# Four-layer graph network on one core: linear before aggregation in layer 0, counting sort on TensorE, 128-row cells, and a regrouped edge loop

## What is computed

```python
# layer 0
h_self = h @ W_self.T
neigh_mean = segment_sum(h[src], dst) / maximum(deg, 1)
x += layernorm(h_self + neigh_mean @ W_neigh.T + bias) * gamma + beta
# layer 1: two graph convolutions with edge weights, then row-normalised
# layer 2: message per edge from h[src] and 128 attributes, sum by dst, GRU cell, batch norm
m = relu(concat(h[src], edge_attr) @ W1.T + b1) @ W2.T + b2
agg = segment_sum(m, dst)
# layer 3
x += segment_sum(h[src] * edge_weight1, dst) @ W_3.T + b_3
```

## Time and profile before

| | |
|---|---|
| time, three runs | 1702.89, 1706.38 (median), 1710.26 us |
| profiled execution, first to last instruction | 1705.3 us |
| DVE / PE / POOL / ACT busy | 1190.8 / 1349.3 / 812.9 / 610.3 us |
| mean granted TensorE clock | 0.924 |
| to the first cell scatter | 104 us |
| the build | 367 to 663 us |
| the edge loop | 1021 to 1366 us |

### The profile page before, as it was taken

One profiled execution on the slowest core, in us unless ns is written; L12 is line 12 of the kernel. 1 busy time (PEld: TensorE's weight loads), 2 busy tenths in 40 slices (PEclk: granted clock), 3 DMA queues, 4 the chain that ended last, 5 costly groups with the idle time before them and its releaser, 6 DMA issues.

```text
span 1705.3 us, 20878 instructions
## 1 busy us (share of the span) xinstructions
PE 1349.3 (79%) x4114; PEld 711.6 (42%) x4114; DVE 1190.8 (70%) x1940; ACT 610.3 (36%) x1561; POOL 812.9 (48%) x985
## 2 busy tenths in 40 slices
PE   0277190039999999599899887899899899999899
PEld 0243140024444443344587533444444344444575
DVE  8999863029999999645624727788888756666632
ACT  0132010037666672000200116777777622222310
POOL 2547776766666665066766615666666500000000
PEclk9989585569999999699999999999999999999899
DMA  8363131010000004333432536756666600000220
GB/s 349 129 249 114 61 113 38 1 31 0 0 0 0 0 0 159 133 96 108 123 90 86 158 129 210 242 176 183 181 188 187 192 31 1 0 1 0 62 86 36
DMA packets 81183, 168.18 MB, mean 99 GB/s; under 512 B 15436, under 2 KB 37838, under 8 KB 77556
## 3 DMA queue, kind: packets, MB, share of 16 engines
q1 hardware_dynamic: 53140, 103.63, 17.5%
q0 software_dynamic: 25472, 59.97, 12.4%
q10 hardware_dynamic: 2528, 4.06, 0.9%
HBM read 116.17 MB, written 51.44 MB: 98 GB/s over the span
## 4 chain that ended last, share of the span: by engine, by line
PE 40%; issue 25%; POOL 15%; DVE 10%; DMA 7%; POOLq 1%; SPq 1%; ACT 1%; DVEq 0%; ACTq 0%
PE pb L985 16%; PE pb L936 16%; POOL dst_rows L654 7%; POOL cell_rows L607 5%; PE pb L1170 4%; DMA arena<-p_rows,gidx 3%; DVE arena L1378 3%; DMA arena<-dst_rows 3%; DVE arena L1233 2%; POOL arena L676 1%; PE pb L922 1%; DVE arena L1261 1%; DVE arena L1228 1%; PE pb L1107 1%; DVE arena L1341 1%
## 5 line engine op out<-in xcount | busy, mean ns | idle before, releaser
L676 POOL DMA_INDIRECT arena<-p_rows,gidx x184 | 188.4, 1024 | 103.3 <-issue 54.6
L985 PE MATMUL pb<-arena 128*128 128x384 f32 x368 | 140.8, 507 | 117.1 <-POOL arena L627 109.1
L654 POOL DMA_INDIRECT dst_rows<-ering,gidx x168 | 168.1, 1001 | 127.2 <-issue 73.6
L607 POOL DMA_INDIRECT cell_rows<-tiles,gidx x168 | 169.8, 1011 | 73.6 <-issue 45.9
L1107 PE MATMUL pb<-arena 128*128 128x512 f32 x368 | 196.6, 617 | 1.3 <-ACT arena L821 1.3
L717 ACT ACTIVATE arena<-iota,cellm 128x128 f32<-128x128 f32 x368 | 127.7, 394 | 194.0 <-DMA cellm<-cell_rows 113.5
L1462 DVE TENSOR_TENSOR arena<-pb,arena 128x512 f32<-128x512 f32 x184 | 126.5, 687 | 65.6 <-DMA arena<-p_rows,gidx 59.6
L1347 DVE TENSOR_TENSOR arena<-iota,cellm 128x256 f32<-128x256 f32 x92 | 107.6, 1170 | 87.6 <-issue 87.6
L985 PEld LDWEIGHTS pb<-arena 128*128 128x128 f32 x368 | 64.1, 192 | 193.1 <-ACT arena L722 166.3
L985 PE MATMUL pb<-tiles,arena 128*128 128x384 f32 x368 | 140.1, 504 | 5.7
L827 ACT ACTIVATE high<-arena 128x512 fp32r<-128x512 f32 x184 | 115.3, 627 | 72.0 <-DVE arena L1462 59.0
(11 more groups left out here) (206 smaller groups left out, 2351.2 us busy)
## 6 DMA issues: line engine op xcount, KB each, us to landing
dst_rows<-arena SPq DMA_DIRECT2D x6, 2046.0 KB, 18.1
arena<-dst_rows SPq DMA_DIRECT2D x46, 264.0 KB
ering<-in_edge_attr_dram SPq DMA_DIRECT2D x41, 256.0 KB
arena<-adj SPq DMA_DIRECT2D x10, 640.0 KB, 4.0
arena<-in_x_dram SPq DMA_DIRECT2D x18, 256.0 KB, 5.2
arena<-in_L_gnn_W_hh_dram SPq DMA_DIRECT2D x3, 1024.0 KB
wt_hh<-ws SPq DMA_DIRECT2D x3, 1024.0 KB, 5.9
arena<-in_L_gnn_W_ih_dram SPq DMA_DIRECT2D x3, 1024.0 KB
```

What stands on the lines that cost most here:

```text
L607: nc.gpsimd.indirect_dma_start(cell_rows[:, :], bass.IndirectOffsetOnAxis(gidx[:, k:k + 1], 0), cring[:, k, :], None).then_inc(c_scattered ...
L654: nc.gpsimd.indirect_dma_start(dst_rows[:, :], bass.IndirectOffsetOnAxis(gidx[:, k:k + 1], 0), ering[:, k, :], None).then_inc(e_scattered[ ...
L676: nc.gpsimd.indirect_dma_start(rows[:, k, :], None, p_rows[:, :], bass.IndirectOffsetOnAxis(gidx[:, k:k + 1], 0)).then_inc(g_landed[k], 16)
L985: ins = nc.tensor.matmul(pb[place][:, 0:3 * P], ohs[:, 2 * place + k], ohd(2 * place + k, 1).rearrange("p a m d -> p (a m d)"), start=k == ...
```

## The change

Six things, all in one step:

1. **Sort by counting on PE.** The one-hot (now column by bucket, bf16) is made in four parts. PE counts it with 68 bf16 products, then for each of 34 spans of 5 columns makes every edge's place in seven products (`rank_span`). DVE multiplies by the one-hot and reduces, 505 elements each. Indices come in five batches of 2, 4, 8, 10 and 10 spans.
2. **128-row cells.** Cells are padded to 128 rows: 272 single chunks in the place of 184 pairs. One-hots and weights are still made for two chunks at once; PE and DVE do one product and one addition a chunk.
3. **Scatters.** The cell scatter goes by spans of five in two halves of a ring. 32 of the 168 edge columns are scattered inside the build, one after the second weighting of each turn of four (`weights_turn` with a column).
4. **Layer 0 linear first.** `zs` = h W_neigh is made beside `ys`, and stored in the place of h0; the sum over neighbours is then directly the result, without turn and product. beta is added to x once, gamma and the norm are fused, relu moves to ACT, the second half of the degrees goes between the tiles.
5. **Order.** W1h is loaded from ACT's queue. b2 is spread by DVE. Matrices are zeroed tile by tile beside `ys`.
6. **Edge loop.** Ring of 16 row chunks (the second half in `ws[:, 1]`), indices copied by fours and between the gathers of the four before, table values loaded once a turn, and every fourth chunk summed in plain float32 without a remainder. `rows_turn(0)` is issued halfway through `p2`.

```diff
-CELL_PAIRS = (E + CELLS * (PAIR - 1)) // PAIR
-CELL_CHUNKS = 2 * CELL_PAIRS
+CELL_CHUNKS = (E + CELLS * (P - 1)) // P
+CELL_CHUNKS = -(-CELL_CHUNKS // 8) * 8
+SPAN = 512 // (CELLS + 1)
+SPANS = -(-J // SPAN)
+WIDE = 2 * GROUP
+WHOLE = 3
+EARLY = CELL_CHUNKS // TURN // COL
...
+        O_PARTS = [0, 9, 18, 27, SPANS]
+        BATCHES = [0, 2, 6, 14, 24, SPANS]
...
+            def scatter_span(i, a, prepare_next, n=SPAN):
+
+                pool.wait_ge(cells_indexed, 2 * i + a + 1)
+                passed()
+                for k in range(n):
+                    nc.gpsimd.indirect_dma_start(cell_rows[:, :], bass.IndirectOffsetOnAxis(gidx[:, SPAN * a + k:SPAN * a + k + 1], 0),
+                                                 cring[:, a, k], None).then_inc(c_scattered[a][k], 16)
+                if prepare_next:
+                    prepare_next()
...
+            def weights_turn(i, with_column=None):
+                for q in range(TURN // 2):
+                    pool.wait_ge(dst_hot, TURN // 2 * i + q + 1)
...
+                    if q == 1 and with_column is not None:
+                        scatter_column(with_column)
...
+            for i in range(COL * EARLY, CELL_CHUNKS // TURN):
                 weights_turn(i)
...
+            def gather_quarter(i, q, prepare_next):
+
+                pool.wait_ge(g_ready, WIDE // 4 * i + q + 1)
+                passed()
+                for k in range(4 * q, 4 * q + 4):
+                    if k % 2 == 0:
+                        at_least(pool, summed, WIDE * i + k - 6)
+                        passed()
+                    if k % 4 == 2 and prepare_next:
+                        prepare_next()
+                    k = k % GROUP
+                    nc.gpsimd.indirect_dma_start(rows[:, k, :], None, p_rows[:, :],
+                                                 bass.IndirectOffsetOnAxis(gidx[:, k:k + 1], 0)).then_inc(g_landed[k], 16)
...
+            def rank_span(g):
+
+                b = to_dve(("slot", g))
+                n = columns(g)
+                nc.tensor.matmul(b[:, 0:n * B1], below, hot_span(g, n), start=True, stop=False)
+                for k in range(1, n):
+                    nc.tensor.matmul(b[:, k * B1:n * B1], ones_b, hot_span(g, n - k), start=False, stop=False)
+                for part in (base_hi, base_lo):
+                    ins = nc.tensor.matmul(b[:, 0:n * B1], row_of[:, g], part.unsqueeze(1).to_broadcast([P, n, B1]),
+                                           start=False, stop=part is base_lo)
+                ins.then_inc(for_dve, 1)
...
+                    for k in range(TURN):
+                        at_least(pe, block_added, TURN * i + k - 3)
...
+                        nc.tensor.matmul(pb[k % 4][:, 0:3 * P], ohs[:, k], ohd(k, 1).rearrange("p a m d -> p (a m d)"),
+                                         start=True, stop=True).then_inc(block_done, 1)
...
                 linear(("ys", t), [(hT[:, t % 2], ws[:, 1])], D)
+                linear(("zs", t), [(hT[:, t % 2], ws[:, 0])], D)
...
+                if whole:
+                    nc.tensor.matmul(sums, hot.bitcast(F32), rows[:, k % GROUP], start=False, stop=True).then_inc(summed, 1)
...
+                for q in range(TURN // 2):
+                    add_block(i, 2 * q, at[2 * q])
+                    if not last or q < TURN // 2 - 3:
+                        hots(i + (q + 3) // 4, (q + 3) % 4)
+                    add_block(i, 2 * q + 1, at[2 * q + 1])
...
+            for t in range(6):
+                degree(1, t)
...
+                read(("y0", t), lambda b: vstt(y, b[:], invc[:, t:t + 1], y, ALU.mult, ALU.add))
+                link(nc.vector.bn_stats(stats[:], y))
+                link(nc.vector.bn_aggr(one_mv[:], stats[:]))
+                inverse_root(("y0", t), one_rstd[:], vts(one_rstd[:], one_mv[:, 1:2], LN_EPS, None, ALU.add))
+                link(vstt(y, y, one_mv[:, 0:1], vec[:, 1], ALU.subtract, ALU.mult))
```

More of the change, by code:

```diff
@@ new lines, in _ @@
+            for n in range(len(BATCHES) - 1):
+                first, last = BATCHES[n] // 2, BATCHES[n + 1] // 2 - 1
+                final = n == len(BATCHES) - 2
+                pool.wait_ge(order_ready[0], n + 1)
+                passed()
+                index_span(first, 0)
+                if last > first:
+                    with pool.Fori(first, last) as i:
+                        scatter_span(i, 0, lambda: index_span(i, 1))
+                        scatter_span(i, 1, lambda: index_span(i + 1, 0))
+                scatter_span(last, 0, lambda: index_span(last, 1, rest if final else SPAN))
+                scatter_span(last, 1, None, rest if final else SPAN)
@@ L662, in _, with scatter_edges @@
+            def scatter_edges(i, q, last=False):
+                prepare_edges(i, q)
+                edges_there(i, q, last)
+                for k in range(4 * q, 4 * q + 4):
+                    scatter_column(k)
+            with pool.Fori(EARLY, turns - 1) as i:
+                scatter_edges(i, 0)
+                scatter_edges(i, 1)
+            scatter_edges(turns - 1, 0)
+            scatter_edges(turns - 1, 1, True)
             pool.wait_ge(h_ready, 2 * NT)
```

851 lines of the change are left out of this document (479 added, 372 removed).

## The result

The changed kernel takes 1505.31 us (median of four runs, 1493.98 to 1506.68) against 1704.64 (four runs, 1702.62 to 1710.26): a ratio of 0.8815, 95% interval 0.878 to 0.885. The forecast was 1494. The profiled execution has a span of 1503.9 against the forecast sum of 1493. Ratios are taken from fast runs alone; a run more than 1.5% above the fastest of its kernel counts as slow, which here are two of e10's six. Single stages are compared by their ends in one profile each. The same stage differs by up to 5 us between executions of code that is the same there (build end to first `x1` sum 144.1 to 148.8, the loop's messages 309.3 to 314.0), so smaller differences say nothing by themselves.

A forecast was written before the change was run, and what follows sets the result against it. No engine was taken to bound the whole, so stages were added along the engine ending each: 553 + 132 + 162.5 + 306 + 339.5 = 1493 us, 1494 against the median of runs. The range was 1445 to 1560.

The forecast's parts named there:

- the 3% on top of the rule: Cell scatter: the 245 us from the per-group rule raised to 253, as the old scatter took 257 against 249.
- The slack is 45 us: Cell scatter: PE's remaining work, with ys/zs till about 255, is over 45 us before the scatter ends at 300.
- 136 cycles are 218: Build: cycles of two chunks stay at 1.60 us, so the 136 without edge columns' cost take 218.
- The step on what sets the cycle: Build: POOL's weighting of 1.04 and its 0.56 idle for DVE's one-hots set the cycle, 1.60 us.
- put tile 9 at 108: Layer 0: nine tiles, four reductions (9.2) and dinv (1.6) place tile 9 at 108 us in the stage.
- land at 107: Layer 0: W1, W2 and W1h, loaded at about 102 us after PE's last sum, arrive at 107.
- half a microsecond for a copy that nothing waits for: Edge loop, POOL by fours: 4 x 1.28 plus this index copy gives 1.4 us a chunk.
- (a): Build dearer by whole columns (+25) and broken cycle (+34), or late columns hold the gathers: 1515 to 1560, chance 0.20.
- (b): Edge loop keeps 1.85 a chunk because gathers, not index loads, are late: +38, 1532, chance 0.12.
- (c): Build runs at 1.04 + 0.38, DVE getting ahead at each column, and edge loop at 1.56: 1454, chance 0.10.
- (d): Layer 0 gains nothing, DVE's tile being as long as PE's was: 62 lost, 1556, chance 0.05.
- (e): Edge loop: PE idles enough to stay at 1.2 GHz, 3.1 us a chunk: +264, 1758, chance 0.02.

The follow-up runs named there:

- e10: Changed kernel with e1, e2 and e6 together, and b1's load for p2 issued by ScalarE instead of SP: 1516.94 us, ratio 0.8853.
- e8: Changed kernel with cell columns scattered in groups of 4 instead of 5 (42 spans): one run, 1507.84 us.
- e1: Changed kernel with ScalarE issuing the last ys load ahead of the W1, W2 and W1h loads, these behind tile 8's root: 1497.51 us, ratio 0.8784.
- e6: Changed kernel with no edge columns scattered inside the build, all 168 after it: one run, 1494.14 us.
- e9: Changed kernel with edge-loop indices copied by twos, each copy with its own wait; ring of 16 and unsplit quarter kept: 1534.47 us, ratio 0.9009.
- e11: e10 plus ScalarE copying turned tiles 0 and 1 of h1 in front of tile 9's second root: 1514.65 us, ratio 0.8881.
- e5: Changed kernel without two thirds of the build's additions, 128 columns a chunk instead of 384, leaving matrices incomplete: one run, 1495.98 us.
- e7: Changed kernel with 320 chunks of cells instead of 272, the 48 more being empty: one run, 1545.23 us.
- e2: Changed kernel with 16 index columns instead of 8 for the edge loop's gathers: 1497.97 us, ratio 0.8771.
- e12: Changed kernel with e1, e2, the copies of e11, and PE's products for the second order one weight block later: 1479.49 us, ratio 0.8673.
- e3: Changed kernel with every edge-loop chunk split into a high and a low part: 1508.53 us, ratio 0.8854.
- e4: Changed kernel with SP loading edge-loop rows as with a ring of 8, except the first 16 chunks: 1634.55 us, ratio 0.9567.

## Why the prediction was right, and where it wasn't

The total was right, and so was what most stages wait for. Luck has a part in the total: 12 us gained in the head stand against 25 lost in layer 0 and the edge loop, and the chances gave such a cancellation 0.01. No experiment takes apart what the head and layer 0 gained; that counting on PE and the linear ahead of the sum gave it is read from the stages' rows.

**Head.** Right in its mechanism (43 against 46; POOL's pace set the end; e8 shows the group's own share). The 12 us over the forecast are 3 at the first scatter, 7 in the scatter, where the 3% on top of the rule didn't come back (246 against its 245), 1.4 up to the first weighting, and one of rounding (46 + 253 is 299, not 300). Wrong in a sentence that cost nothing in the changed kernel's profile: "The slack is 45 us". With 9 us from the last `zs` product to the build it was 29 in the one profile, 5 to 6 in e1 and e6, and in e9, e10 and e11 there was none; the prediction's own sign of being wrong, `zs` not over at 300, came up in e9 and e10. I had added up PE's work at its own durations and left out that DVE, PE and the clock hold each other up in the order's products.

**Build.** 246 against 244.5, by luck, out of two errors that cancel. "136 cycles are 218": the bare build took 232 (e6), because one cycle in four waits for PE. 16 and 10 for 32 columns and their preparations: together 12.6, because a column falls beside that wait. The step on what sets the cycle is shown by e5, the saving per chunk by e7. A column costs 0.39 with its preparations, so no one-hot is kept out for a whole one. The Trainium skill's port rule (same page and section), read so that a scatter counts as reading SBUF, would have made it 25 us more; e6 doesn't agree with that reading, which isn't the section's own either: it takes descriptor generation to need the write side of the ports and calls that inferred.

**Layer 0.** 132 against 145.5. The steps "put tile 9 at 108" (it started at 113.7) and "land at 107" took ACT's queue for free. The loads of W1, W2 and W1h hold a root and the last `ys` load (6 us, e1), and the copies of `h1` stand behind the last relu (6.3 us between e10 and e11). With both undone the stage took 132.3, the forecast's number (whose last step is loose: 107 and ten tiles of 2.2 are 129, not 131). The start of tile 0 (44 forecast, 44.7) and of tile 8 (102, 101.8) were right to a microsecond. I had counted ACT's instructions, and not what stands behind what.

**Layer 1.** 162.5 against 162.0, and the edge scatter's last column 243.8 us after the build against 243 (its first 27.4 instead of 31, then 1.60 a column instead of 1.56). That W1h's load is worth nothing isn't tested by itself.

**Edge loop.** 306 against 317.5, all of it in the pace, 1.71 instead of 1.64. PE's terms came true where it doesn't wait (1.43 for a split chunk, 1004.98 to 1006.41, and 1.82 for a whole one, 1001.72 to 1003.54). The failed step is "half a microsecond for a copy that nothing waits for", and with it the 0.10 for semaphores and late gathers: the copy itself waits, for the gathers of four before (37.7 us in 30 times), and makes the next ones late. Taking that wait away gave 8 us in e2 and 11 in e12, nearly the forecast pace, and nothing in e10 and e11, so it is a part of the 11.5 us and its size isn't settled. What the forecast called DVE's need, 1.35, isn't what sets the pace, since splitting the whole chunks changes the loop by less than its scatter (e3). Of the 28 us gained, indices by fours gave 13 on the ring of 16, and on a ring of eight fours are 128 us dearer than on one of 16 (e4).

**Rivals.** (a), (b) and (c) asked for a build, a loop or a cycle that wasn't there. (b) named the right suspect, late gathers, at 38 us; what e2 and e12 took back is 8 to 11. (d), layer 0 gaining nothing, was out: it gained 48. (e), a TensorE kept at its lower level, didn't come in the edge loop, where the clock stayed at 0.97. Something like it came in a place where I hadn't looked, the sort, where gaps and lower clock go together with a build that begins 16 us later in e9 and 22 in e10.

## What to carry to other kernels

When work is moved, read the queue it lands on in order and ask what stands behind it: the losses found here (the last `ys` load behind ACT's weight loads, SP's stores behind edge loads, gathers behind POOL's index copy) were each an instruction held by a wait that it had no use for, and two were mended by moving a line or widening a buffer by 24 bytes a partition (the second in two executions of four). A ring and the size of the pieces taken from it are one decision: fours gave 13 us over twos on a ring of 16, and on one of eight they made the loop 128 us longer than on 16, and so some 99 longer than before the change. A slack read from one execution is one sample; where two lines of work end close together, shorten the hidden one too.

## What the runs showed of the hardware that I hadn't expected

An indirect DMA of POOL costs the build 0.39 us, preparations included, because it falls into waits of POOL that are there anyway (e6 against the changed kernel), and 1.28 with its gap when there are none (1.58 with preparations and without the long wait for loads, e6). The one-hot's duration in the profile (1.21 before, 0.45 changed, 0.95 in e5, and 0.38 alone) tells when it was issued, not what it costs: in all three kernels it ends 0.27 to 0.29 us after POOL's operation. PE had gaps of up to 3.7 us (e5) without a recorded cause in the order's products, in eleven of the thirteen profiles of kernels that sort this way (3 us in sum in e8, 7 to 12 in the others), and in e10 the mean clock from 120 to 145 us was then 0.54; four bf16 products of 404 columns or less took 0.60 us at the higher level and 1.05 at the lower.
